# Own-chunk values of an attention layer computed transposed, with the head mask summed by ScalarE and VectorE

## The chip, the cores and the metric

The kernel runs on one core of a Trainium2 chip. The metric is the device time of one launch in microseconds (us), lower is better.

## The reference

Four layers follow one another. The first two are a scan layer with a gate and eight small experts, the third is a linear attention over 16 heads, the fourth is a gated cell that carries a state through 16 batches of 512 tokens of 128 features. Only the attention's sum over earlier tokens is touched:

```python
scores = jnp.einsum('bthd,bshd->bhts', Q, K) * S ** (-0.5)
Wmat = scores * jnp.transpose(decay, (0, 3, 1, 2)) * jnp.transpose(lam_ts, (0, 2, 1, 3))
Y = jnp.einsum('bhts,bshd->bthd', Wmat, V).reshape(Bb, Tt, H * HD)
o = Y @ Wout.T + x
```

H is 16 heads, a head's value has 8 features (HD), lam_ts depends on the level of the pair (t, s) in a binary tree. The part in which t and s lie in the same chunk of 32 tokens is what is changed here.

## The kernel before

A batch is four tiles of 128 tokens. The kernel is written engine by engine, with every wait spelled out as a semaphore. Each engine runs `stages(i, j)`, in which the attention and cell of batch i are interleaved with the scan and expert layers of batch j = i + 1: once for batch 0, 14 times in a hardware loop, then `last()` for batch 15. The order in each engine's queue is the order written in its `stages`; it is in this order that a waiting instruction holds up all that stands behind it.

**The attention of one batch.** Pairs across chunks go through node matrices: `levels` (L733 and L737 on TensorE, PE) makes products that VectorE (DVE) weights (`level_products`, L1732) and sums (`level_total`, L1739). Pairs in the same chunk: `pair_scores` (L702) gives scores, `pair_weights` (L1718) multiplies them in place into `pair`, 128 partitions of (chunk, s) by 16 heads x 32 tokens for each tile. Then for each tile n
- `chunk_values` (L748): four matmuls, four heads each, with `pair` as the stationary operand and `vbd` moved, a copy of the values in which each chunk has its own columns (filled by four ScalarE copies of 32 partitions, L1149). The result holds (head, token) on partitions, and of its columns only those of the partition's own head are wanted;
- `own_heads` (L1750): DVE multiplies the 512 columns by a head mask into `ym`;
- `chunk_sums` (L756): four matmuls with a matrix of ones sum the four heads away, so that tokens stand on partitions;
- `tile_sum` (L1761): DVE adds the level sums, into `yt`.

`turn_out` (L765) transposes `yt`, ScalarE (ACT) copies it (L1203), `project_out` (L771) multiplies with Wout, and `attention_out` (L1766) adds the skip path. `norm2` (L1467 with skip as output) normalises the batch before; GpSimd (POOL) then runs `finish` and `residual(i)`, and `sum0` (L1573) waits for the latter.

**The steps around it.** PE runs `levels(i, 3)`, which waits for `level_products(i, 2)`, and directly behind it `out0(j)` (L559 to L563). `sum0` and `norm1` on DVE follow, then `turn_x1` (L574) on PE, the gates of the cell (L784 to L793), the copy x1Th on ACT (L1095, waits for the third gate), `low_part` (L1587) on DVE, `values` (L582 to L590) on PE, the cell, the next `norm0` and its two short ACT steps (L1014), the gates `gates1` up to `g_ready`, `running_sums` (L634 and L637), `token_sums` (L1677), and so on to `delta` on DVE (L1531), for which `scan_b` (L501 with MBCl) waits. `heads` (L626 to L628) are 48 matmuls per batch in split fp32 (high and low part as fp32r), each with an ACT copy (L1115). `deltas` (L493) is one plain fp32 matmul per batch; the trace counts every plain fp32 matmul as two instructions.

**Start and end.** `node_vectors` builds small coefficient columns on DVE at the end of `first()`; POOL's `split_weights` (L2026, L2028) makes the high and low parts of five weight blocks before the loop. At the end POOL and DVE add the last outputs (L2064, L1799) and SyncE (SP) stores them; the two halves of batch 15 wait for `last_out` (L1906) behind `last_norm` (L1896).

```python
for g in range(4):
    at = 512 * n + 128 * g
    mm = pe.matmul(tile(P1[3], g), pair[:, at:at + 128], vbd[:, at:at + 128], start=True, stop=True)
```

Of the kernel before, what the change touches and what calls it, by code (L numbers as in the profile page):

```python
# [29 lines left out]
NODES = 32  # L30
EPS = 1e-5
# [33 lines left out]
def build(nc, x, weights, consts, out):  # L65
# [9 lines left out]
    with ExitStack() as ctx:  # L75
# [50 lines left out]
        Mdelta = sb("Mdelta", 128)  # L126
# [69 lines left out]
        with nc.sbuf_tensor("cellh", [128, T], fp32r) as cellh, nc.sbuf_tensor("celll", [128, T], fp32r) as celll:  # L196
# [9 lines left out]
        vbd = sb("vbd", TILES * 512)  # L206
# [6 lines left out]
        ym = sb("ym", 2 * 512)  # L213
        dts = pair[:, 0:12 * 64]
        lvs = sb("lvs", 128)
        cgt = lvs[:, 0:64]
# [23 lines left out]
        P1 = [psum(f"p1_{n}") for n in range(5)]  # L240
# [13 lines left out]
            s_ps lam_ps dlam_ready w_ready vbd_zero vbd_ready y1_ps ym_ready y2_ps lev_ps lev_ready levsum_ready  # L254
# [31 lines left out]
        def _(sp):  # L286
# [49 lines left out]
            def last():  # L336
# [16 lines left out]
                for b in (0, 1, 2, 3, 4, 7, 8, 9, 10, 5, 6, 11, 12):  # L353
                    if b in END_POOL:
                        sp.wait_ge(R["end_pool_add"], END_POOL.index(b) + 1)
                    else:
                        sp.wait_ge(R["end_add"], END_DVE.index(b) + 1)
                    store(b, whole, end_hx[b])
                for half in range(2):
                    sp.wait_ge(R["end_add"], len(END_DVE) + 1 + half)  # L360
                    store(B - 1, slice(2 * half, 2 * half + 2), end_hx[B - 1])
                    sp.wait_ge(R["end_pool_add"], END_POOL.index(13 + half) + 1)
                    store(13 + half, whole, end_hx[13 + half])
# [5 lines left out]
        def _(pe):  # L369
# [122 lines left out]
            def deltas(j):  # L492
                pe.matmul(P0[0][:, :], Mdelta[:, :], xnT[:, :], start=True, stop=True).then_inc(R["delta_ps"], 1)  # L493
# [17 lines left out]
            def scan_x(j):  # L511
                if later(j):
                    pe.wait_ge(R["wsplit_steps"], 10)
# [20 lines left out]
            def gate_u(j, q):  # L534
# [7 lines left out]
                else:  # L542
                    pe.wait_ge(R["hsplit_ready"], 2 * j)
# [33 lines left out]
            def values_in_parts(j):  # L577

                pe.wait_ge(R["x1P_ready"], j + 1)
                for n, free in enumerate(("dlam_ready", "ym_ready", "yt_ready", "x1Th_ready")):  # L580
                    pe.wait_ge(R[free], j + 1 if n == 3 else 4 * j)
                    pe.matmul(P1[(2 + n) % 5][:, 336:VDW], tile(x1P, n), w("Wvdw", 336, VDW), start=True, stop=True)  # L582
                pe.wait_ge(R["wsplit_steps"], 10)
# [9 lines left out]
            def values(j):  # L593
# [5 lines left out]
                for n, free in enumerate(("dlam_ready", "ym_ready", "yt_ready", "x1Th_ready")):  # L599
# [30 lines left out]
            def running_sums(i):  # L630
# [3 lines left out]
                pe.matmul(P1[2][:, 0:64], upto[:, :], g, start=True, stop=False)  # L634
                pe.wait_ge(R["gsum_steps"], 2 * i + 2)
# [104 lines left out]
            def chunk_values(i, n):  # L740
                if n > 0:
                    pe.wait_ge(R["ym_ready"], 4 * i + n)
# [3 lines left out]
                for g in range(4):  # L746
                    at = 512 * n + 128 * g
                    mm = pe.matmul(tile(P1[3], g), pair[:, at:at + 128], vbd[:, at:at + 128], start=True, stop=True)  # L748
                mm.then_inc(R["y1_ps"], 1)

            def chunk_sums(i, n):
                if n > 0:
                    pe.wait_ge(R["yt_ready"], 4 * i + n)
                pe.wait_ge(R["ym_ready"], 4 * i + n + 1)
                for c in range(4):
                    mm = pe.matmul(P1[4][32 * c:32 * c + 32, 0:128], k("sum_heads"),  # L756
                                   view(tile(ym, n % 2, 512), "p (g c v) -> p g c v", g=4, c=4)[:, :, c, :],
                                   start=True, stop=True)
                mm.then_inc(R["y2_ps"], 1)
# [28 lines left out]
            def recur_cell(i, n):  # L788

                pe.wait_ge(R["csplit_ready"], 2 * i + 2)  # L790
# [5 lines left out]
            def stages(i, j):  # L796
# [41 lines left out]
                if i is not None:  # L838
                    chunk_sums(i, 0)
# [8 lines left out]
                if i is not None:  # L848
                    chunk_sums(i, 1)
# [5 lines left out]
                if i is not None:  # L855
                    chunk_sums(i, 2)
                if i is not None:
# [3 lines left out]
                if i is not None:  # L861
                    chunk_values(i, 3)
                    if j is not None:
# [1341 lines left out]
```

## Time and profile before

| | |
|---|---|
| median of 3 runs | 1022.07 us (1021.91 to 1022.53) |
| profiled execution, own time | 1022.31 us |
| its span, first to last instruction | 1020.5 us |
| PE busy | 969.2 us (95%) |
| DVE busy | 858.9 us (84%) |
| ACT busy | 704.3 us (69%) |
| POOL busy | 254.9 us (25%) |
| granted TensorE clock, mean | 0.990 |

Busy time counts overlapping matmuls once. Some 1.8 us of the profiled execution lie outside the span.

### The profile page before, as it was taken

How to read it: one execution, taken by the hardware profiler on the slowest of the kernel's cores; microseconds unless marked ns; L12 is line 12 of the kernel's file. 1: busy time of each engine (PE TensorE's matmuls, PEld its weight loads, DVE VectorE, ACT ScalarE, POOL GpSimd, SP SyncE). 2: the span in 40 equal slices, each digit the busy share in tenths (PEclk: the TensorE clock that was granted, in tenths of full speed). 3: DMA queues.
4: the chain of work that ended last, by engine and by line, in shares of the span. 5: the costliest groups of instructions: out<-in, count | busy, mean ns of one | idle time of the engine just before them, and what ended most of it. 6: DMA issues, size and time to landing. Idle time of an engine off the chain costs nothing. (4 is left out here: it accounts for less than half of the span.)

```text
span 1020.5 us, 20931 instructions
## 1 busy us (share of the span) xinstructions
PE 969.2 (95%) x6894; PEld 708.1 (69%) x6894; DVE 858.9 (84%) x2156; ACT 704.3 (69%) x1528; POOL 254.9 (25%) x319
## 2 busy tenths in 40 slices
PE   6879999999999999999999999999999999999995
PEld 3656767767676777768677676766767677776763
DVE  6888797988979798897979979798897979889777
ACT  4575784939579494866939577593957849396684
POOL 0042021220222122021312212132122212202367
PEclk9989999999999999999999999999999999999997
DMA  4000000000000000000000000000000000000526
GB/s 159 18 4 1 22 2 23 8 21 10 0 31 0 21 10 10 21 0 31 0 21 10 0 31 0 31 0 21 10 0 31 0 21 10 10 21 0 196 77 202
DMA packets 31909, 27.62 MB, mean 27 GB/s; under 512 B 1553, under 2 KB 25745, under 8 KB 31761
## 3 DMA queue, kind: packets, MB, share of 16 engines
q1 hardware_dynamic: 31888, 27.37, 8.3%
q8 instruction: 11, 0.18, 0.1%
q14 instruction: 10, 0.07, 0.0%
HBM read 15.57 MB, written 11.80 MB: 27 GB/s over the span
## 5 line engine op out<-in xcount | busy, mean ns | idle before, releaser
L1115 ACT ACTIVATE gx<-p 128x512 f32<-128x512 f32 x256 | 146.5, 597 | 2.1 <-PE p L628 0.5
L626 PE MATMUL p<-x1Th,Gl 128*128 128x512 f32 x256 | 107.7, 421 | 0.0
L628 PE MATMUL p<-x1Th,Gh 128*128 128x512 f32 x256 | 101.4, 396 | 0.0
L627 PE MATMUL p<-x1Tl,Gh 128*128 128x512 f32 x256 | 100.6, 393 | 0.0
L1979 POOL TENSOR_TENSOR vp<-vdw,e 128x256 f32<-128x256 f32 (+3 forms) x80 | 55.1, 724 | 162.3 <-DVE ms L1663 162.3
L1063 ACT ACTIVATE gelu<-p,bias_u 128x512 f32<-128x512 f32 x32 | 22.0, 688 | 105.3 <-PE p L550 105.3
L748 PEld LDWEIGHTS p<-vbd,pair 128*128 128x128 f32 x512 | 62.0, 191 | 40.4 <-issue 26.8
L748 PE MATMUL p<-vbd,pair 128*128 128x128 f32 x512 | 73.3, 286 | 0.0
L2040 POOL TENSOR_TENSOR skip<-skip,W 128x512 f32<-128x512 f32 x15 | 19.2, 1279 | 215.4 <-DVE skip L1467 215.4
L688 PEld LDWEIGHTS p<-rs,GT 128*128 128x128 f32 x512 | 60.7, 191 | 16.8 <-ACT ms L1198 14.6
L1069 ACT ACTIVATE sm<-mv 128x4 f32<-128x4 f32 x31 | 6.3, 204 | 91.4 <-DVE mv L1462 91.0
L702 PE MATMUL p<-gx,x1T 128*32 128x512 f32 x512 | 67.8, 602 | 0.2 <-DVE pair L1718 0.2
L1991 POOL TENSOR_TENSOR xnTl<-xnT 128x1 fp32r<-128x1 f32 x15 | 2.9, 194 | 248.6 <-DVE pair L1618 248.6
L688 PE MATMUL p<-rs,GT 128*128 128x120 f32 x512 | 63.8, 278 | 0.2 <-ACT ms L1198 0.2
L1704 DVE TENSOR_TENSOR pair<-pair,p 128x512 f32<-128x512 f32 x64 | 42.5, 684 | 24.9 <-PE p L719 24.9
L628 PEld LDWEIGHTS p<-x1Th,Gh 128*128 128x128 f32 x256 | 48.3, 189 | 11.0
L1198 ACT ACTIVATE ms<-p 128x120 f32<-128x120 f32 x256 | 46.9, 287 | 11.3 <-PE p L688 8.8
L626 PEld LDWEIGHTS p<-x1Th,Gl 128*128 128x128 f32 x256 | 48.7, 190 | 8.3 <-ACT gx L1115 0.7
L627 PEld LDWEIGHTS p<-x1Tl,Gh 128*128 128x128 f32 x256 | 48.7, 190 | 7.6
L1750 DVE TENSOR_TENSOR ym<-p,K 128x512 f32<-128x512 f32 x64 | 43.7, 683 | 2.7 <-PE p L748 2.7
L737 PE MATMUL p<-ms,x1T 128*128 128x128 f32 x256 | 45.5, 300 | 0.0
L1739 DVE TENSOR_REDUCE lvs<-lv 128x128 f32<-128x256 f32 (+1 forms) x64 | 43.2, 675 | 2.2
(340 smaller groups left out, 2855.6 us busy)
## 6 DMA issues: line engine op xcount, KB each, us to landing
xin<-in_x SPq DMA_DIRECT2D x16, 256.0 KB, 2.8
hx_scratch<-vdw SPq DMA_DIRECT2D x15, 256.0 KB, 2.6
res_scratch<-normed SPq DMA_DIRECT2D x14, 256.0 KB, 2.0
gx<-in_weights SPq DMA_DIRECT2D x1, 1216.0 KB, 9.4
vp<-hx_scratch SPq DMA_DIRECT2D x4, 256.0 KB, 3.8
GT<-res_scratch SPq DMA_DIRECT2D x4, 256.0 KB, 3.4
out<-vp SPq DMA_DIRECT2D x4, 256.0 KB, 3.5
W<-in_weights SPq DMA_DIRECT2D x1, 746.0 KB, 10.5
```

What stands on the lines that cost most here:

```text
L626: pe.matmul(head_bank(h)[:, :], tile(Gl, h), x1Th[:, :], start=True, stop=False)
L627: pe.matmul(head_bank(h)[:, :], tile(Gh, h), x1Tl[:, :], start=False, stop=False)
L628: pe.matmul(head_bank(h)[:, :], tile(Gh, h), x1Th[:, :], start=False, stop=True).then_inc(R["gx_ps"], 1)
L688: mm = pe.matmul(bank[:, 120 * a:120 * a + 120], tile(GT, h), view(rs[:, 0:1920], "p (n c) -> p n c", c=128)[:, :, HD * h:HD * h + HD], st ...
L702: mm = pe.matmul(P1[1][32 * c:32 * c + 32, :], x1T[:, 128 * n + 32 * c:128 * n + 32 * c + 32], view(gx[:, :], "p (h t) -> p h t", h=H)[:, ...
L737: mm = pe.matmul(bank[:, 128 * (a + 1):128 * (a + 2)], tile(x1T, n), node(m), start=True, stop=True)
L748: mm = pe.matmul(tile(P1[3], g), pair[:, at:at + 128], vbd[:, at:at + 128], start=True, stop=True)
L1115: act.activation(tile(gx, h, T), head_bank(h)[:, :], ACT.Copy).then_inc(R["gx_copied"], 1)
L1198: cp = act.activation(dst[:, at], src[:, at], ACT.Copy)
L1739: dve.tensor_reduce(lvs[:, :], view(lv[:, 0:128 * count], "p (l v) -> p v l", l=count), AX.X, ALU.add)\
L1750: dve.tensor_tensor(view(tile(ym, n % 2, 512), "p (m a e) -> p m a e", m=16, a=4), view(P1[3][:, :], "p (m a e) -> p m a e", m=16, a=4), s ...
L1979: last = pool.tensor_tensor(view(vp[:, at:at + 128 * count], "p (s h e) -> p s h e", s=count, e=HD), spread(v.unsqueeze(1), [128, count, H ...
```

## The change

The own-chunk product is taken with the operands exchanged. The values are now the stationary operand (64 partitions of two chunks by 32 columns, four heads of 8), `pair` moves with the weights of four heads (128 columns), and 16 matmuls per tile write features on partitions and tokens on columns, in the two banks `y1`. Each partition needs one of four column blocks, the one of its own head: ACT takes the first with a mask as its scale (`first_part`), DVE adds the three others (`other_parts`). The result `yc` is already transposed, so the level sums go alone through `turn_out`, and DVE adds `yc` after it (`turned_out`) in place of the ACT copy. `vbd` is filled by two ACT copies of 128 partitions. With it: `deltas` becomes three fp32r matmuls with a broadcast column, the running sums are cut in two around a head, `left_ends` goes ahead of `deltas`, `turn_out` ahead of the gates, `norm2` ahead of the third tile; part of `node_vectors` and the POOL splits move into stage 0; the end of the kernel keeps its last tiles in PSUM and stores in another order.

```diff
+PARTS = 4
+PASSES = 4 // PARTS
...
+        y1 = ctx.enter_context(nc.psum_tensor("p1_34", [128, 1024], fp32))
+        P1 += [y1[:, 0:512], y1[:, 512:1024]]
+        def quadrant_part(a):
+            return view(y1[:, :], "p (h x) -> p h x", h=2)[:, :, 64 * a:64 * a + 64]
+        def by_token(ap):
+            return view(ap, "p (h x) -> p h x", h=2)
...
             def deltas(j):
+                column = lambda t: spread(t[:, 0:1], [128, 128])
...
+                pe.wait_ge(R["wsplit_steps"], 6)
+                pe.wait_ge(R["xsplit_ready"], 2 * j)
+                pe.matmul(P0[0][:, :], column(Mdl), xnTh[:, :], start=True, stop=False)
+                pe.matmul(P0[0][:, :], column(Mdh), xnTl[:, :], start=False, stop=False)
+                pe.matmul(P0[0][:, :], column(Mdh), xnTh[:, :], start=False, stop=True).then_inc(R["delta_ps"], 1)
...
             def chunk_values(i, n):
                 if n > 0:
-                    pe.wait_ge(R["ym_ready"], 4 * i + n)
+                    pe.wait_ge(R["yc_ready"], 4 * i + n)
...
-                for g in range(4):
-                    at = 512 * n + 128 * g
-                    mm = pe.matmul(tile(P1[3], g), pair[:, at:at + 128], vbd[:, at:at + 128], start=True, stop=True)
+                width = CHUNK * PARTS
+                for c in range(2):
+                    for b in range(PASSES):
+                        for half in range(2):
+                            rows = slice(64 * half, 64 * half + 64)
+                            for g in range(4):
+                                at, of = 32 * (((4 * n + g) * 2 + c) * PASSES + b), 512 * n + 128 * g + width * b
+                                to = view(P1[3 + half][32 * g:32 * g + 32, 0:2 * width], "p (a c t) -> p a c t", a=PARTS, c=2)
+                                mm = pe.matmul(to[:, :, c], vbd[rows, at:at + 32],
+                                               view(pair[rows, of:of + width], "p (a t) -> p a t", a=PARTS),
+                                               start=(b == 0), stop=(b == PASSES - 1))
...
-            def chunk_sums(i, n):
...
                     heads(i, 7, 8)
+                    carried_sums(i)
                 if j is not None:
                     logits(j)
+                if i is not None:
+                    left_ends(i)
+                if j is not None:
                     deltas(j)
                 if i is not None:
-                    left_ends(i)
                     heads(i, 8, 12)
...
                     chunk_values(i, 3)
+                    turn_out(i)
...
-                    chunk_sums(i, 3)
...
-                    turn_out(i)
...
+            def first_part(i, n):
+                act.wait_ge(R["y1_ps"], 4 * i + n + 1)
+                act.activation(by_token(yu[:, :]), quadrant_part(0), ACT.Copy, scale=head_part[:, 0:1]).then_inc(R["yu_ready"], 1)
...
-            def own_heads(i, n):
...
-            def tile_sum(i, n):
...
+            def other_parts(i, n):
+                dve.wait_ge(R["yu_ready"], 4 * i + n + 1)
+                for a in range(1, PARTS):
+                    if a > 1:
+                        dve.wait_ge(R["yc_steps"], (PARTS - 2) * (4 * i + n) + a - 1)
+                    last = dve.scalar_tensor_tensor(by_token(tile(yc, n)), quadrant_part(a), head_part[:, a:a + 1],
+                                                    by_token(yu[:, :] if a == 1 else tile(yc, n)), ALU.mult, ALU.add)
+                    last.then_inc(R["yc_ready" if a == PARTS - 1 else "yc_steps"], 1)
+
+            def turned_out(i):
+                dve.wait_ge(R["ytT_ps"], i + 1)
+                dve.wait_ge(R["yc_ready"], 4 * i + 4)
+                dve.tensor_tensor(ytT[:, :], P1[1][:, :], yc[:, :], ALU.add).then_inc(R["ytT_ready"], 1)
...
-                    own_heads(i, 0)
                     pair_weights(i, 1)
+                    other_parts(i, 0)
                     level_sum(i, 0)
-                    tile_sum(i, 0)
                 if j is not None:
                     gate0(j, 0)
...
                     gate0(j, 1)
                 if i is not None:
-                    own_heads(i, 2)
-                    level_sum(i, 2)
                     if later(i):
                         norm2(i - 1)
+                    other_parts(i, 2)
+                    level_sum(i, 2)
                     pair_weights(i, 3)
-                    tile_sum(i, 2)
                     level_sum(i, 3)
...
+            last_ob = P1[3]
...
+            def split_scan_weights():
+
+                pool.wait_ge(R["z1_ps"], 1)
+                pool.wait_ge(R["xh_ready"], 2)
+                split_weights(((Mdh, Mdl, Mdelta[:, :]), (Winh, Winl, w("Win")), (MBCh, MBCl, MBC[:, :])), 0)
+
+            def split_other_weights():
+
+                pool.wait_ge(R["u1_ps"], 1)
```

The lines left out: `node_vectors` now runs ahead of `gates_low_part` in `first()`; its second half, `node_coefficients`, with five short instructions more for the new masks, runs in stage 0 ahead of `fold_own`. ACT's `stages` calls `first_part(i, n)` ahead of the gate's tanh, between tanh and gelu, between the two gelus, and behind them. In `last()` ACT copies the first head ahead of `rstd2` and runs `lam_logs` behind the fourth, the last output tile of batch 15 is built in the bank `P1[3]` (in L1879, L1896, L1906), and SP stores batches 13 and 14 ahead of the two halves of batch 15.

## Rows read from the trace of the kernel before

**Rows 1.** The page, busy time by engine.
```profile
PE 969.2 (95%) x6894; PEld 708.1 (69%) x6894; DVE 858.9 (84%) x2156; ACT 704.3 (69%) x1528; POOL 254.9 (25%) x319
```

**Rows 2.** Groups of PE: count | busy us, mean ns | idle before, releaser.
```profile
L748 PE MATMUL p<-vbd,pair 128*128 128x128 f32 x512 | 73.3, 286 | 0.0
...
L719 PE MATMUL p<-nodesT,K 32*32 32x512 f32 x512 | 34.8, 599 | 0.4 <-DVE pair L1704 0.4
...
L756 PE MATMUL p<-ym,K 128*32 128x128 f32 x512 | 27.3, 284 | 6.1 <-DVE ym L1750 6.1
```

**Rows 3.** Groups of DVE.
```profile
L1750 DVE TENSOR_TENSOR ym<-p,K 128x512 f32<-128x512 f32 x64 | 43.7, 683 | 2.7 <-PE p L748 2.7
...
L1761 DVE TENSOR_TENSOR rs<-lvs,p 128x128 f32<-128x128 f32 x64 | 18.3, 286 | 12.6 <-PE p L756 9.4
```

**Rows 4.** Timeline of DVE in one period: start us, us, what [idle before].
```profile
503.37 0.69 DVE L1704 TENSOR_TENSOR pair<-pair,p 128x512 f32<-128x512 f32 x1 [0.92 <-PE p L719]
...
507.07 1.28 DVE L1704 TENSOR_TENSOR pair<-pair,p 128x512 f32<-128x512 f32 x2 [0.35 <-PE p L719]
...
521.84 0.61 DVE L1732 TENSOR_TENSOR lv<-p,alpha 128x256 f32<-128x256 f32 x2
...
523.00 1.11 DVE L1467 TENSOR_SCALAR skip<-skip,mv,sm 128x128 f32<-128x128 f32 x4
...
528.43 0.69 DVE L1573 TENSOR_TENSOR x<-p,xin 128x512 f32<-128x512 f32 x1 [1.82 <-POOL res L1965]
...
535.66 0.69 DVE L1587 TENSOR_TENSOR x1Tl<-x1T,x1Th 128x512 fp32r<-128x512 f32 x1 [1.90 <-ACT x1Th L1095]
...
553.82 0.68 DVE L1531 SCALAR_TENSOR_TENSOR decay<-p,sp 128x512 f32<-128x512 f32 x1
```

**Rows 5.** Timeline of PE in the same period.
```profile
522.70 0.44 PE L733 MATMUL p<-ms,x1T 128*64 128x128 f32 x4
...
523.85 0.39 PE L559 MATMUL p<-W,y 128*128 128x128 f32 x2
...
527.75 0.22 PE L563 MATMUL p<-b_b,oh_b 128*128 128x128 bf16 x1
...
532.38 0.63 PE L574 MATMUL p<-K,xn 128*128 128x128 f32 x4 [0.68 <-DVE xn L1467]
...
545.88 0.42 PE L637 MATMUL p<-pair,ones 128*128 128x48 f32 x2 [0.41 <-DVE pair L1624]
...
547.37 1.13 PE L493 MATMUL p<-xnT,Mdelta 128*128 128x512 f32 x2
...
554.97 0.39 PE L501 MATMUL p<-xnTh,MBCl 128*128 128x512 f32 x1
...
555.66 0.39 PE L501 MATMUL p<-xnTh,MBCl 128*128 128x512 f32 x1
```

**Rows 6.** Timeline of ACT in the same period.
```profile
535.03 0.60 ACT L1095 ACTIVATE x1Th<-p 128x512 fp32r<-128x512 f32 x1 [0.48 <-PE p L793]
...
540.56 0.21 ACT L1014 ACTIVATE sm<-sm 128x4 f32<-128x4 f32 x1 [0.43 <-DVE sm L1482]
```

**Rows 7.** Timelines at the start: DVE twice, then PE.
```profile
49.42 1.27 DVE L1413 SCALAR_TENSOR_TENSOR K<-K 128x128 f32<-128x128 f32 x1
...
53.59 3.04 DVE L1467 TENSOR_SCALAR xn<-xin,mv,sm 128x128 f32<-128x128 f32 x4
...
56.78 1.08 PE L467 MATMUL p<-K,xn 128*128 128x128 f32 x4 [5.50 <-DVE xn L1467]
```

**Rows 8.** Timelines at the end: DVE twice, then POOL, then SP's queue.
```profile
1012.62 2.16 DVE L1896 SCALAR_TENSOR_TENSOR skip<-skip,mv,W 128x128 f32<-128x128 f32 x2
...
1015.40 0.61 DVE L1896 SCALAR_TENSOR_TENSOR skip<-skip,mv,W 128x128 f32<-128x128 f32 x2
...
1013.11 1.26 POOL L2064 TENSOR_TENSOR W<-W,normed 128x512 f32<-128x512 f32 x1
...
1017.16 0.49 SPq L333 DMA_DIRECT2D out<-W  x1
```

More of the change, by code:

```diff
@@ L358, in last @@
                     store(b, whole, end_hx[b])
+                for b in (13, 14):
+                    sp.wait_ge(R["end_pool_add"], END_POOL.index(b) + 1)
+                    store(b, whole, end_hx[b])
                 for half in range(2):
@@ L1219, in end_tanh @@
                 act.activation(END_BANKS[turn][:, :] if b in END_DVE else end_hx[b], end_hx[b], ACT.Tanh).then_inc(R["end_tanh"], 1)
-            def last_copy(half, bank):
-                act.wait_ge(R["ytT_ps"], B + half)
-                act.activation(ytT[:, 256 * half:256 * half + 256], bank[:, 0:256], ACT.Copy).then_inc(R["ytT_ready"], 1)
             def last_rstd(half):
@@ L1280, in stages @@
                 gelus()
+                if i is not None:
+                    first_part(i, 0)
                 if j is not None:
@@ L1405, in node_vectors, with node_coefficients @@
                 step(last)
+            def node_coefficients():
+                step(dve.tensor_tensor(chunk_part[:, :], k("own_chunk", 0, 2), k("own_chunk", 2, 4), ALU.add))
+                for a in range(PARTS):
+                    step(dve.tensor_reduce(head_part[:, a:a + 1], view(k("diag"), "p (b x) -> p b x", b=PASSES)[:, :, 8 * a:8 * a + 8],
+                                           AX.XY, ALU.add))
                 step(dve.memset(ones_to[:, 0:1], 1.0))
@@ L1445, in first @@
                 later_weights()
+                node_vectors()
                 gates_low_part()
@@ L1737, in level_total @@
                 dve.wait_ge(R["lev_ready"], 4 * i + n + 1)
+                if n == 0 and later(i):
+                    dve.wait_ge(R["ytT_ps"], i)
                 count = sum(r[2] for r in level_runs(n))
-                dve.tensor_reduce(lvs[:, :], view(lv[:, 0:128 * count], "p (l v) -> p v l", l=count), AX.X, ALU.add)\
-                    .then_inc(R["levsum_ready"], 1)
+                dve.tensor_reduce(tile(yt, n), view(lv[:, 0:128 * count], "p (l v) -> p v l", l=count), AX.X, ALU.add)\
+                    .then_inc(R["yt_ready"], 1)
             def level_sum(i, n):
@@ L1818, in stages @@
                     lam_sum(i)
+                    if not later(i):
+                        node_coefficients()
                     fold_own(i)
@@ L1848, in stages @@
                 if i is not None:
-                    own_heads(i, 1)
                     pair_weights(i, 2)
+                    other_parts(i, 1)
                     level_sum(i, 1)
-                    tile_sum(i, 1)
                 if j is not None:
@@ L1866, in stages @@
                 if i is not None:
-                    own_heads(i, 3)
-                    tile_sum(i, 3)
+                    other_parts(i, 3)
+                    turned_out(i)
                 if j is not None:
@@ L1872, in stages, with last_turned @@
                     recurrence(i)
+            last_ob = P1[3]
+            def last_turned(half, bank):
+                cols = slice(256 * half, 256 * half + 256)
+                dve.wait_ge(R["ytT_ps"], B + half)
+                dve.wait_ge(R["yc_ready"], 4 * (B - 1) + 2 * half + 2)
+                dve.tensor_tensor(ytT[:, cols], bank[:, 0:256], yc[:, cols], ALU.add).then_inc(R["ytT_ready"], 1)
             def last_attention_out(half):
@@ L1884, in last_stats @@
                 for n in (2 * half, 2 * half + 1):
-                    last = dve.bn_stats(st2[:, 6 * n:6 * n + 6], tile(ob, n))
+                    last = dve.bn_stats(st2[:, 6 * n:6 * n + 6], tile(last_ob, n))
                 last.then_inc(R["st2_ready"], 1)
@@ L2083, in stages @@
             def stages(i, j):
+                if not later(i):
+                    split_scan_weights()
                 split_inputs(j)
@@ L2086, in stages @@
                 split_rows(i, j)
+                if not later(i):
+                    split_other_weights()
                 split_cell(i, 2 * i + 2)
```

145 lines of the change are left out of this document (66 added, 79 removed).

## The prediction

> **What bounds the kernel now.** I read the busy times first: PE has 95% and DVE 84% of the span [rows 1], so PE looks like the bound. The groups of PE by line then show what the change can take from it, and their idle column that PE waits for DVE there, 6.1 us in all before L756 [rows 2]. Last the timelines of the three engines over one period, to see which wait ends last. The reader is to see two stretches. From 507.07 DVE works without a gap until level_total of tile 3 [rows 4], and PE runs just behind it: `out0` starts at 523.85 [rows 5]. From `out0` to the copy x1Th the batch is one chain through PE, DVE and ACT, with idle time on each (1.82, 0.68, 1.90 us [rows 4, 5]). So both engines are at their limit in the first stretch, and in the second latency counts, not load. A faster PE gets only as far as DVE's queue lets it.
>
> **PE, removed and added.** One tile's `chunk_values` takes 73.3 / 64 = 1.15 us and its `chunk_sums` 27.3 / 64 = 0.43 [rows 2], together 6.3 us per batch. The new product issues 32 instructions per tile (16 fp32 matmuls of two) on eight places of the array, two row halves by four column groups. The nearest row for eight places is L719: 16 instructions of 512 columns take 34.8 / 32 = 1.09 us, so eight run at once. For 128 columns the nearest is L756: eight instructions on four places, two rounds, in 0.43. Four rounds of eight then cost about twice that less one start, 0.65 us; if only four ran at once, eight rounds, 1.4 us; a quarter of L719's time scaled, 0.5, is the lower end. I take 0.65, as L719 has both row and column places. By TensorE: Matmul & The Clock Gate, The mechanism, of the Trainium skill, weights load beside running matmuls only where the row groups differ, which would put the four column groups of one half in a row and the price at the upper end. L756 lies all in one row group and still takes 0.43 for eight, so I leave the price.
>
> `deltas` is 1.13 us busy now [rows 5]. Three fp32r matmuls start 0.23 apart (the six from 554.97 to 555.66 and on: 0.69 for three [rows 5]), about 0.8 with the start: 0.2 less. PE thus loses some 3.9 us of work per batch, 60 us over the kernel. What follows says how much of it arrives.
>
> **ACT.** The four masked first parts cost about 0.3 us each and lie in its waits for the gate; `own_values` falls from four instructions to two and the copy of `ytT` goes. Nothing here is on the path; if it were, the two would nearly cancel. Cost taken as nothing, cover: ACT waits behind norm statistics and gelu, 69% busy [rows 1].
>
> **DVE, where the sum is made.** `own_heads` is 0.683 us long [rows 3], but independent instructions of 512 columns follow one another every 0.60 (two in 1.28 [rows 4]). `tile_sum` is 0.286 [rows 3] and with the gap before it adds 0.38. In their place stand three dependent instructions of 128 columns with a pointer scalar. The nearest is L1896, two in 0.61 [rows 8]: 0.35 long, 0.26 apart when independent. Dependent, each of the first two costs 0.35 + 0.04, the last 0.26: 1.04 per tile. Bounds: 0.28 each without the pointer's share gives 0.85; 0.45 each, should two banks in one operand cost more, gives 1.3. Up to `level_products` of tile 2, DVE now does 3 x 1.04 instead of 3 x 0.60 + 2 x 0.38, +0.56, and the moved `norm2`, 1.02 of its 1.11 [rows 4], stands ahead of it: +1.6. In the old order it ends at 521.84 + 0.61 = 522.45 [rows 4] and PE takes `levels(3)` at 522.70 [rows 5]; in the new one both are at 524.1. PE, some 3 us early, waits, and `out0` stands behind that wait. **`out0` is 1.4 us late.**
>
> **What the rest of the period gives back.** Each as a shift against the old timeline:
> - `sum0`: `out0` ended at 527.75 + 0.22 = 527.97, `sum0` began at 528.43 behind POOL's `res` [rows 4, 5]. POOL is started by `norm2`, now earlier, so 0.4 is given back: +1.0. The same for `turn_x1` (532.38 [rows 5]). `chunk_values(3)` and `turn_out` fit ahead of it: 0.65 + 0.43 instead of 1.1, with 0.68 idle.
> - The third gate follows without the 0.36 of `chunk_sums(3)`: +0.64 for x1Th (535.03 [rows 6]) and `low_part` (535.66 [rows 4]). The moved `turn_out` would take 0.43 more off `values`, but its fourth block waits for x1Th: heads enter at about +0.3.
> - The cell and `norm0` follow on DVE; ACT's next gated step, idle 0.43 before it at 540.56 [rows 6], comes at +0.57, and so does `g_ready`.
> - PE no longer idles 0.41 before L637 [rows 5], since a head stands between, but the head (0.7) delays the sums by 0.3: `token_sums` at +0.87. PE itself is level with the old timeline here, with the 0.2 of `deltas`.
> - `delta` on DVE ends at 553.82 + 0.68 = 554.50 [rows 4], at +0.87 is 555.37. `scan_b` was at 554.97 [rows 5]. PE waits: **+0.45**. DVE's own 0.87 vanishes in its 0.92 idle at 503.37 [rows 4], PE's 0.45 does not.
>
> So a period is 0.45 us longer, and 14 of them and the last half one make +6.6 us.
>
> **Start.** PE waits 5.50 us for xn of batch 1 at 56.78 [rows 7], behind `node_vectors` (its last piece at 49.42) and four normalising instructions that take 3.04 instead of 1.11 while POOL splits weights [rows 4, 7]. Both leave that place. But `node_coefficients`, some 4.1 us with its five new instructions, comes back ahead of `fold_own` in stage 0, where DVE has under 1 us idle, and POOL's split now stands beside the gates, where it can hold DVE as it did before. Gain 2.0 us, between 0 and 4. By the GPSIMD Engine Reference of the Trainium skill POOL contends with Vector instructions that have two SBUF inputs; the gates have such ones, so by the rule the stall moves rather than ends, and 2 rather than 4 is right.
>
> **End.** The last store is issued at 1017.16 [rows 8], behind the halves of batch 15, though POOL is done at 1013.11 + 1.26 = 1014.37. It now goes ahead. On DVE the three-part sums add 0.3 in all plus two sums of 0.33, while `last_norm` reads PSUM: 0.61 instead of 2.16 [rows 8]; DVE also had waits at the start of its last tiles. It ends about 1.6 us earlier, and the last store moves by 2.4 us (1.2 if the 2.16 stays).
>
> **Sum.** Against the profiled execution, 1022.31 us: + 6.6 - 2.0 - 2.4 = 1024.5; the median is 0.24 lower, so 1024.3 us.
>
> **Rivals.**
> - *The three-part sum is cheap (faster).* With 0.85 per tile the shift of `out0` is 0.8, the pause at `scan_b` goes, and a period is about 0.15 shorter: 14.5 x -0.15 = -2.2, with start and end -6.6: about 1015.5. For it: dependent short steps elsewhere on DVE cost little more than their length. Against: the pointer's 0.07 shows in L1896. It decides at 0.90 per tile, where a period is unchanged; start and end alone then give 1017.9. Chance 0.33, with all cases below 1020.
> - *The DVE chain costs more (clearly slower).* 1.3 per tile: + 0.8 on `out0` and as much per period, about 1033. Chance 0.1.
> - *Four places at once, not eight.* 1.4 us per tile: hidden in tiles 0 to 2 by PE's new slack, but `chunk_values(3)` stands between `out0` and `turn_x1`, and passes the 0.68 idle by 0.4: +6, about 1030. Chance 0.05.
> - *PE's saving arrives* because DVE has a gap I don't see: a third of 60 us, about 1005. Chance 0.03. DVE's unbroken stretch speaks against it.
> - *Nothing much*: loop +2 to +6 cancelled by start and end, 1020 to 1024. Chance 0.22.
>
> **Numbers.** 0.2% is 2 us, about what a measurement of this kernel can tell. Slower by more, with my forecast, 0.44; within, 0.22; faster, 0.34. Eight in ten: from 1013 to 1031, which takes in the cheap sum and leaves out the 1.3 and the full saving.
>
> **What would show it.** In the changed profile PE should idle before `levels` of tile 3, about 3 us per batch, with DVE's `level_products` as the releaser, and a little before `scan_b`, released by `delta`. Its busy share falls to about 88%. The 32 instructions of a tile should span 0.65 us plus tails, the three DVE instructions 1.04. `sum0` should wait for PE instead of POOL, the first xn on PE should come 4 to 5 us earlier, and the last store should be of batch 15. The prediction is wrong at its root if PE doesn't wait at `levels(3)`, and in its size if the three-part sum isn't 1.04.

## The result, and the profile after

The changed kernel takes 1053.51 us, the median of four runs (1052.30 to 1055.19), against 1022.28 us for the kernel before in the same rounds (1021.91 to 1022.53): a ratio of 1.0304, 95% interval 1.0288 to 1.0321. It is 3% slower. The forecast was 1024.3 us with a range up to 1031.0, so the true time lies far outside. One of the four runs of e1 below (1031.58 us) and one of the kernel before beside it (1070.28 us) were slow ones, at a granted clock of 0.85: the medians count them, the ratios don't.

The page of the changed kernel gives busy times, and below them the clock that TensorE was granted, slice by slice.

```profile
span 1051.7 us, 23196 instructions
PE 951.7 (90%) x7933; PEld 692.3 (66%) x7933; DVE 877.1 (83%) x2242; ACT 698.8 (66%) x1543; POOL 254.0 (24%) x321
...
PEclk9989999999999998999999999998999999899997
```

The summary by core (us from first to last instruction, mean granted clock):

```profile
core 0: 1051.7 us, clock 0.957
```

PE's share fell from 95% to 90% [rows 1], yet its busy time fell only 17.5 us, not the 60 us that the prediction takes out. The mean clock is the first thing to see: 0.957, where the kernel before had 0.990. The page's digits nearly hide it, since a short fall is averaged over a slice of 26 us.

The groups of PE and DVE (count | busy us, mean ns | idle before):

```profile
L782 PE MATMUL p<-pair,vbd 64*32 64x128 f32 x2048 | 43.7, 279 | 0.4
L760 PE MATMUL p<-ms,x1T 128*64 128x128 f32 x256 | 30.4, 317 | 47.0 <-DVE lv L1771 47.0
L524 PE MATMUL p<-xnTh,MBCl 128*128 128x512 f32 x60 | 25.3, 422 | 0.4 <-DVE decay L1568 0.4
...
L1792 DVE SCALAR_TENSOR_TENSOR yc<-p,head_part,yc 128x128 f32<-128x128 f32 x128 | 44.9, 350 | 4.5
```

`chunk_values` costs 43.7 / 64 = 0.68 us a tile instead of 1.15 [rows 2], and `chunk_sums` is gone. In their place stands the wait of `levels` (L760): 47.0 us for DVE's level values, 3.15 us in each of 14 batches, as forecast, and 1.64 and 1.21 in the first and the last.

The same moments as in [rows 4, 5], one batch of the changed kernel: DVE (L1741 is the reference, at 507.07 before), then PE.

```profile
521.56 1.28 DVE L1741 TENSOR_TENSOR pair<-pair,p 128x512 f32<-128x512 f32 x2 [0.35 <-PE p L746]
...
535.81 1.11 DVE L1504 TENSOR_SCALAR skip<-skip,mv,sm 128x128 f32<-128x128 f32 x4
536.84 0.34 DVE L1792 SCALAR_TENSOR_TENSOR yc<-p,head_part,yu 128x128 f32<-128x128 f32 x1
537.22 0.74 DVE L1792 SCALAR_TENSOR_TENSOR yc<-p,head_part,yc 128x128 f32<-128x128 f32 x2
537.87 0.61 DVE L1771 TENSOR_TENSOR lv<-p,alpha 128x256 f32<-128x256 f32 x2
...
545.35 0.69 DVE L1610 TENSOR_TENSOR x<-p,xin 128x512 f32<-128x512 f32 x1 [2.62 <-PE p L587]
```

```profile
538.62 0.69 PE L760 MATMUL p<-ms,x1T 128*64 128x128 f32 x4 [3.15 <-DVE lv L1771]
539.25 1.65 PE L764 MATMUL p<-ms,x1T 128*128 128x128 f32 x6
540.69 0.63 PE L583 MATMUL p<-W,y 128*128 128x128 f32 x2
...
543.14 0.44 PE L583 MATMUL p<-W,y 128*128 128x128 f32 x2
```

PE waits 3.15 us, and then the same instructions are longer: L760 takes 0.69 us where it took 0.44 [rows 5], and L583 takes 0.63 in its first pair and 0.44 two rounds later. Stretches of the same batch (us | busy PE, PEld, DVE, ACT, POOL | PEclk) say why:

```profile
534.00:538.30 4.30, 1.47 (x11) 0.98 (x11) 4.12 (x12) 1.97 (x2) 1.26 (x1) 1.00 0.00 0
538.30:541.70 3.40, 3.08 (x15) 2.78 (x16) 2.10 (x5) 0.00 (x0) 3.09 (x3) 0.50 0.20 77
541.70:545.30 3.60, 3.60 (x41) 3.41 (x44) 1.03 (x1) 0.00 (x0) 0.00 (x0) 1.00 0.00 0
```

Behind the wait the granted clock is 0.50, that is 1.2 GHz, from 538.3 to 541.7, and 1.00 (2.4 GHz) again afterwards. Each of the 14 waits of 3.15 us has such a fall of the clock, for 3.4 us in nine batches and 6.8 us in five. The five long ones begin 0.5 to 1.1 us before the wait ends, the nine short ones from 0.4 us before its end to 1.0 us behind it. Two more falls of 3.4 us have other places: one at 91.2, behind a wait of 2.31 us of L729 in the first batch, one at 1036.7, behind the 1.21 us of the last. So the loop is longer than anything in the forecast's sum. The group of the transposes that begin each batch's node matrices gives the mean period:

```profile
L1708 DVE STREAM_TRANSPOSE nodesT<-ms x16: 2302/2311/2312, 72.7 to 1015.3; 128x2048 f32<-128x2048 f32 x16
```

(1015.3 - 72.7) / 15 = 62.84 us. The kernel before has (982.4 - 73.1) / 15 = 60.62:

```profile
L1671 DVE STREAM_TRANSPOSE nodesT<-ms x16: 2302/2312/2314, 73.1 to 982.4; 128x2048 f32<-128x2048 f32 x16
```

Leaving out the first and the last, single periods are 60.44 to 60.49 us before; after they are 62.2 to 62.4 with a short fall of the clock and 63.4 to 63.7 with a long one.

### The profile page after: what moved, and what is told of

Its sections match the earlier page's. It is cut to its first block and busy times, and to the rows that moved or that the text cites. A ratio compares the mean times of both kernels' runs of the same rounds, so it can differ in the third digit from the quotient of the medians.

```text
span 1051.7 us, 23196 instructions
## 1 busy us (share of the span) xinstructions
PE 951.7 (90%) x7933; PEld 692.3 (66%) x7933; DVE 877.1 (83%) x2242; ACT 698.8 (66%) x1543; POOL 254.0 (24%) x321
## 5 line engine op out<-in xcount | busy, mean ns | idle before, releaser
L1180 ACT ACTIVATE yu<-p,head_part 128x128 f32<-128x128 f32 x64 | 23.5, 368 | 189.0 <-PE p L782 188.9
L729 PE MATMUL p<-gx,x1T 128*32 128x512 f32 x512 | 68.8, 610 | 15.6 <-DVE pair L1755 15.3
L760 PE MATMUL p<-ms,x1T 128*64 128x128 f32 x256 | 30.4, 317 | 47.0 <-DVE lv L1771 47.0
L715 PEld LDWEIGHTS p<-rs,GT 128*128 128x128 f32 x512 | 60.7, 191 | 15.6 <-ACT ms L1226 13.4
L1741 DVE TENSOR_TENSOR pair<-pair,p 128x512 f32<-128x512 f32 x64 | 42.4, 684 | 23.6 <-PE p L746 23.6
L782 PEld LDWEIGHTS p<-pair,vbd 64*32 64x32 f32 x2048 | 27.1, 107 | 45.0 <-issue 45.0
L764 PE MATMUL p<-ms,x1T 128*128 128x128 f32 x256 | 55.5, 352 | 0.0
L760 PEld LDWEIGHTS p<-ms,x1T 128*64 128x64 f32 x256 | 14.0, 144 | 59.0 <-issue 59.0
L1610 DVE TENSOR_TENSOR x<-p,xin 128x512 f32<-128x512 f32 x16 | 11.1, 691 | 49.7 <-PE p L587 49.7
```

The lines of the kernel that those rows point to most:

```text
L715: mm = pe.matmul(bank[:, 120 * a:120 * a + 120], tile(GT, h), view(rs[:, 0:1920], "p (n c) -> p n c", c=128)[:, :, HD * h:HD * h + HD], st ...
L729: mm = pe.matmul(P1[1][32 * c:32 * c + 32, :], x1T[:, 128 * n + 32 * c:128 * n + 32 * c + 32], view(gx[:, :], "p (h t) -> p h t", h=H)[:, ...
L760: pe.matmul(bank[64 * c:64 * c + 64, 0:128], x1T[:, 128 * n + 64 * c:128 * n + 64 * c + 64], node((2 * n, 8 + n)[c]), start=True, stop=True)
L764: mm = pe.matmul(bank[:, 128 * (a + 1):128 * (a + 2)], tile(x1T, n), node(m), start=True, stop=True)
L782: mm = pe.matmul(to[:, :, c], vbd[rows, at:at + 32], view(pair[rows, of:of + width], "p (a t) -> p a t", a=PARTS), start=(b == 0), stop=(b ...
L1741: dve.tensor_tensor(tile(pair, n, 512), tile(pair, n, 512), P1[(2, 0)[n % 2]][:, :], ALU.mult)\
```

## The experiments

Theory T: PE's wait of 3 us ahead of `levels(3)`, made by the order of DVE's queue, makes the clock fall, and that is most of the loss. R1: the clock falls for another reason and DVE's longer queue is the loss. R2: the new form of matmul (64 x 32 places) lowers the clock. The ratio is to the kernel before in the same rounds. In the table "period" is that of steady batches without a fall / with a 3.4 us one, "falls" counts them in the loop's last 14 periods, and the wait is PE's longest that recurs in them. e7 leaves out a part of the sum, so its output is another one; all the others compute the same.

| kernel | median us | ratio to before, 95% | PE's wait | falls | period |
|---|---|---|---|---|---|
| before | 1022.28 | 1 | 0.7 | 0 | 60.46 |
| changed | 1053.51 | 1.0304 (1.0288 to 1.0321) | 3.15 | 14 | none / 62.38 |
| e1, reordered | 994.75 | 0.9731 (0.9711 to 0.9750) | 1.10 | 0 | 58.69 |
| e2, wait filled | 1025.75 | 1.0037 (1.0024 to 1.0050) | 0.77 | 0 | 60.74 |
| e3, norm2 back | 1033.09 | 1.0094 (1.0065 to 1.0122) | 2.13 | 13 | 60.27 / 61.37 |
| e4, old kernel delayed | 1080.80 | 1.0577 (1.0559 to 1.0595) | 2.6 | 11 | 63.40 / 64.50 |
| e5, old kernel reordered | 1056.14 | 1.0323 (1.0305 to 1.0340) | 2.0 | 6 | 62.11 / 63.73 |
| e6, e1 with products first | 1006.09 | 0.9833 (0.9817 to 0.9850) | 0.9 | 0 | 59.43 |
| e7, e1 with one part less | 983.75 | 0.9622 (0.9606 to 0.9638) | 0.8 | 0 | 57.95 |
| e8, wait half filled | 1033.94 | 1.0111 (1.0094 to 1.0128) | 1.72 | 5 | 60.76 / 62.41 |
| e9, e1 with old deltas | 997.12 | 0.9746 (0.9729 to 0.9763) | 1.1 | 0 | 58.81 |
| e10, e1 with norm2 late | 1033.50 | 1.0113 (1.0097 to 1.0128) | 2.19 | 5 | 60.87 / 62.43 |
| e11, e1 again | 995.25 | 0.9739 (0.9726 to 0.9752) | 1.1 | 0 | 58.70 |

### e2: the wait filled with work

```diff
                 if i is not None:
+                    for _ in range(12):
+                        pe.matmul(P1[2][:, :], tile(Gh, 0), x1Th[:, :], start=True, stop=True)
                     levels(i, 3)
```

> Edit: the changed kernel, with 12 fp32r matmuls of 128 columns (tile 0 of Gh by x1Th, into the third bank of P1, which the next batch's values overwrite; the output is unchanged) ahead of levels(3) of each batch, some 2.8 us of work in a wait of 3.15 us. Theory T: PE has more to do and ends its wait at the same moment, but the clock stays at 1.0: a period loses the 1.4 to 2.9 us that the stretches at 0.5 cost, and the kernel takes 1022 to 1030 us. Rival R1 (DVE's longer queue alone costs the time): work laid into a wait changes nothing, 1053 us, or some us more. Rival R2 (the form of the new matmuls lowers the clock): the stretches at 0.5 stay, 1053 us.

The matmuls stream 512 columns each, not 128 as that text calls them. 1025.75 us: adding 3 us of work to the busiest engine in 15 of the 16 batches saves 28 us. The wait and what follows (timeline of PE), then the stretches around it:

```profile
523.16 3.01 PE L884 MATMUL p<-x1Th,Gh 128*128 128x512 f32 x12
526.51 0.44 PE L760 MATMUL p<-ms,x1T 128*64 128x128 f32 x4 [0.34 <-DVE lv L1773]
526.88 0.94 PE L764 MATMUL p<-ms,x1T 128*128 128x128 f32 x6
527.65 0.39 PE L583 MATMUL p<-W,y 128*128 128x128 f32 x2
```

```profile
526.00:529.50 3.50, 3.16 (x28) 2.83 (x28) 3.17 (x6) 0.00 (x0) 3.18 (x4) 1.00 0.19 75
529.50:533.00 3.50, 3.50 (x58) 3.11 (x58) 1.33 (x5) 0.37 (x1) 0.10 (x1) 1.00 0.00 0
```

`levels(3)` is released by the same DVE instruction as in the changed kernel and at the same point of DVE's queue, but now runs at full clock. R1 and R2 both wanted 1053. This run also prices the change without the clock: the period is 60.74 us, 0.28 more than before.

### e4: the wait put into the old kernel

```diff
                 if i is not None:
+                    for n in range(5):
+                        dve.tensor_reduce(pad[:, n:n + 1], spread(w("lng").unsqueeze(1), [128, 4, 128]), AX.XY, ALU.add)
                     own_heads(i, 2)
```

> Edit: the kernel before, with five reductions of 512 columns on DVE (their results go nowhere) ahead of own_heads(2), some 2.8 us. It has none of the 64x32 matmuls. PE then waits some 3 us before levels(3), as in the changed kernel. Theory T: the granted clock falls to 0.5 behind this wait, in the old kernel too, and a period costs 1.4 to 2.9 us more than the delay itself; with 1 to 2.5 us of delay arriving at the end of the period, that gives 60.5 + 2.4 to 5.4 per period, 1058 to 1100 us. R1 (the queue alone): at most the 2.8 us of added work per period, 1022 + 42 = 1064, with the clock at 1.0 in the loop. R2 (the new form of matmul lowers the clock): the clock stays at 1.0 here.

The stretches of one batch of e4, around a wait of 2.62 us ahead of L757 (`chunk_sums`, where the delay of `own_heads` meets PE first; the expectation had placed it at `levels(3)`):

```profile
487.74 0.43 PE L757 MATMUL p<-ym,K 128*32 128x128 f32 x8 [2.62 <-DVE ym L1751]
```

```profile
486.00:489.50 3.50, 1.66 (x19) 1.28 (x20) 3.46 (x10) 1.15 (x1) 0.00 (x0) 1.00 0.00 0
489.50:492.90 3.40, 3.40 (x18) 3.30 (x17) 2.74 (x6) 0.00 (x0) 2.72 (x3) 0.50 0.00 0
```

The old kernel, which has none of the new matmuls, loses the clock in the same way, in 11 of 14 periods. R2 falls here too. Periods without a fall are 2.94 us longer than before (the added work; 1 to 2.5 us of it were expected to arrive), those with one 1.1 us more. R1 had a ceiling of 1064 us; 1080.8 is above it, but most of that is the added work, 15 x 2.94 = 44 of the 58.5 us, and the falls of the clock are 11 x 1.1 = 12. What rules R1 out is the clock at 0.50, not the time alone.

### e1: the order of DVE's queue, and its repeat e11

```diff
                 if i is not None:
+                    level_products(i, 2)
                     if later(i):
                         norm2(i - 1)
+                    level_total(i, 2)
                     other_parts(i, 2)
-                    level_sum(i, 2)
                     pair_weights(i, 3)
```

> Edit: the changed kernel with DVE's queue reordered behind gate0 of the second half: level_products(2) first, then norm2 and level_total(2), then other_parts(2). That brings the level values of tile 2, on which PE waits before levels(3), forward by norm2 and other_parts, 1.02 + 1.03 = 2.05 us. Theory T (PE's wait of 3.15 us there makes the granted clock fall to 0.5 behind it): the wait shrinks to some 1.1 us, TensorE's clock stays at 1.0 in every batch, a period falls from 62.2 to 63.7 us to between 60.0 and 60.7, and the kernel takes 1013 to 1023 us. Rival R1 (the clock falls for another reason, only the longer queue of DVE is undone): the stretches at 0.5 stay, a period gets at most the 2 us of the shorter wait, and the kernel stays above 1030 us. Rival R2 (the 64x32 matmuls themselves lower the clock): as R1, the granted clock stays at about 0.957 on average.

994.75 us, and 995.25 in the repeat, is faster than either theory said. It is 2.7% faster than the kernel before and 5.6% faster than the changed one (994.75 / 1053.51 = 0.944), with the same computation. The summary, the group, and DVE's timeline of one batch:

```profile
core 0: 992.5 us, clock 0.990
```

```profile
L1708 DVE STREAM_TRANSPOSE nodesT<-ms x16: 2300/2311/2314, 71.7 to 956.1; 128x2048 f32<-128x2048 f32 x16
```

```profile
509.16 0.61 DVE L1771 TENSOR_TENSOR lv<-p,alpha 128x256 f32<-128x256 f32 x2
509.69 1.10 DVE L1504 TENSOR_SCALAR skip<-skip,mv,sm 128x128 f32<-128x128 f32 x4
510.71 0.59 DVE L1780 TENSOR_REDUCE rs<-lv 128x128 f32<-128x384 f32 x1
511.21 0.34 DVE L1792 SCALAR_TENSOR_TENSOR yc<-p,head_part,yu 128x128 f32<-128x128 f32 x1
...
515.22 0.69 DVE L1610 TENSOR_TENSOR x<-p,xin 128x512 f32<-128x512 f32 x1 [0.58 <-PE p L587]
```

The level products of tile 2 stand first, 1.02 + 1.03 us earlier. The gain of 31 us over e2 is nearly all this: the period went from 60.74 to 58.69, 2.05 us, what the products moved by, and 15 periods of that are 30.8 us. The expected 60.0 to 60.7 was too high: `sum0` is released by PE 0.58 us after DVE is free, and POOL's `res`, which `norm2` starts early, doesn't hold it.

> The first experiment's kernel once more, unchanged, beside these two in the same rounds: 993 to 997 us, 2.5 to 2.9% under the kernel before.

As expected: 995.25 us.

### e3 and e8: how long a wait the clock bears

```diff
 # e3
-                    if later(i):
-                        norm2(i - 1)
                     other_parts(i, 2)
                     level_sum(i, 2)
+                    if later(i):
+                        norm2(i - 1)
                     pair_weights(i, 3)
 # e8, the diff of e2 with
+                    for _ in range(6):
```

> Edit: the changed kernel with norm2 back in its old place, behind level_sum(2). The level values of tile 2 come 1.02 us earlier, so PE waits some 2.1 us ahead of levels(3), between the 0.25 of the kernel before and the 3.15 of the changed one. Theory T has no row for a wait of this length: either the clock falls as often as now and the kernel gains 0 to 15 us (1038 to 1053), or it falls in fewer batches or none, 1018 to 1030. Rival R1: about 1 us per period less, 1038, with the clock as it is. R2: the same as R1. The run says which waits the clock bears, and tells R1 apart only together with the first and the fourth.

> Edit: as the second experiment, but with 6 dummy matmuls ahead of levels(3) instead of 12 (the changed kernel otherwise), some 1.4 us of work, so PE idles 1.7 us there. The runs so far bear 1.1 us (the clock stays at 1.0) and not 2.1 (the clock falls in nearly every batch, for 3.4 us). Theory T in the form that the idle stretch decides: at 1.7 us either no stretch at 0.5 in the loop, a period of 60.74 us and 1026 us, or one in most batches, about 61.9 us and 1040. Rival (the half clock is cured by the number of matmuls, not by the idle time, in proportion): the stretches at 0.5 last half as long on average, 1040 us. The median alone does not tell these apart; the list of stretches does.

e3, with 2.13 us, falls in 13 of 14 periods; the one without takes 60.27 us, those with 61.37 (leaving out the last, which is some 2 us longer in every kernel). Its 1033.09 us meets neither branch of its expectation: the clock falls about as often as in the changed kernel, yet the gain is 20.4 us and not 0 to 15, since all these falls are short and cost 1.1 us each. e8, with 1.72 us, falls in 5 of 14: those periods have about 62.4 us, again without the last, and the nine others about 60.8. Neither line of the last expectation is met, for the clock falls neither in most batches nor in none. All its falls in the loop last 3.4 us, so the fillers cure some batches wholly and others not at all.

```profile
528.34 0.44 PE L760 MATMUL p<-ms,x1T 128*64 128x128 f32 x4 [1.72 <-DVE lv L1773]
```

```profile
529.10:532.50 3.40, 3.40 (x18) 3.34 (x18) 2.08 (x3) 0.00 (x0) 2.14 (x3) 0.51 0.20 77
```

The length of the one wait isn't the whole rule: e4 with 2.6 us falls less often than e3 with 2.1. Even one program differs from execution to execution: in the first batch of e1 and of its repeat e11 PE waits 2.3 us ahead of L729, and the clock falls behind it at 91.2 in e11 and not at all in e1. What else decides was not separated. That wait and the stretch behind it, e1 first, then e11:

```profile
89.89 1.06 PE L729 MATMUL p<-gx,x1T 128*32 128x512 f32 x8 [2.32 <-DVE pair L1755]
90.50:94.50 4.00, 3.21 (x59) 1.93 (x55) 3.84 (x8) 1.05 (x2) 0.00 (x0) 1.00 0.00 0
```

```profile
90.35 1.13 PE L729 MATMUL p<-gx,x1T 128*32 128x512 f32 x8 [2.30 <-DVE pair L1755]
91.20:94.60 3.40, 3.40 (x46) 2.38 (x43) 3.26 (x7) 0.37 (x1) 0.00 (x0) 0.50 0.00 0
```

### e5: the good order in the old kernel

```diff
-                    own_heads(i, 2)
-                    level_sum(i, 2)
+                    level_products(i, 2)
                     if later(i):
                         norm2(i - 1)
+                    level_total(i, 2)
+                    own_heads(i, 2)
```

> Edit: the kernel before with the queue order of the first experiment: behind gate0 of the second half level_products(2), norm2, level_total(2), then own_heads(2). The question is whether the gain of that order belongs to the change or was to be had without it. Theory D (in the kernel before PE is the bound, waiting only 0.25 us before levels(3); the order pays only where PE has slack): a period falls by 0 to 0.25 us from 60.46, or grows by some tenths as PE's chunk_sums(2) now waits for own_heads(2); 1018 to 1030 us. Rival O (the order alone brought it, and the old kernel would gain as much): a period of 58.7 us, some 995 us.

1056.14 us, worse than both expectations. In the old kernel PE's `chunk_sums(2)` needs `own_heads(2)`, and moved behind, it holds PE where the changed kernel has nothing to wait for:

```profile
L756 PE MATMUL p<-ym,K 128*32 128x128 f32 x512 | 27.3, 283 | 35.1 <-DVE ym L1750 35.1
```

That was 6.1 [rows 2]. So rival O is out: this order gains only together with the change. Another order of the old kernel, say `level_products(2)` first and `own_heads(2)` ahead of `norm2`, was not run, so how much of the 2.7% needs the change isn't settled. In the old kernel this order costs 1.65 us per period without a fall, and the clock falls in 6 of 14 besides.

### e6, e7, e9, e10: what bounds the reordered kernel

e6 puts `level_products(i, 2)` ahead of `gate0(j, 1)` also; e7 loops `for a in (1, 3)` in `other_parts` (its wait between them counts one step per tile instead of two); e9 takes the old body of `deltas`; e10 moves `norm2(i - 1)` behind `pair_weights(i, 3)`.

```diff
 # e6
                 if i is not None:
                     level_products(i, 2)
+                if j is not None:
+                    gate0(j, 1)
 # e7
-                for a in range(1, PARTS):
+                for a in (1, 3):
 # e10
-                    if later(i):
-                        norm2(i - 1)
                     level_total(i, 2)
                     other_parts(i, 2)
                     pair_weights(i, 3)
+                    if later(i):
+                        norm2(i - 1)
```

> Edit: the first experiment's kernel with other_parts summing two of its three masked parts (the one of column group 2 is left out, so the output lacks that part); one DVE instruction of 128 columns less per tile, four per batch. It measures what the three dependent sums are worth where they stand on the path. By the step of the prediction (0.35 + 0.04 us each, two ahead of level_products(2), PE behind it): 0.8 us per period, 57.9 us, 983 us in all. Rival (DVE has slack once the clock holds, PE is the bound again): under 0.2 us per period, 992 to 995 us.

983.75 us and a period of 57.95: 0.74 less for the two instructions ahead of `level_products(2)`, 0.37 each. The prediction's price was 0.39, and nearly all of it is on the path. DVE's queue up to that point bounds the reordered kernel.

> Edit: the first experiment's kernel, with level_products(2) also ahead of gate0 of the second half. In that run PE finishes levels(2) at 507.9 where DVE would ask for it at 507.1, and it waits 1.10 us ahead of levels(3). Expected: that wait of PE goes, DVE gets a new one of about 0.5 us, out0 now waits for gate0 instead and starts 0.1 to 0.7 us earlier; a period of 58.0 to 58.6 us against 58.69, 985 to 993 us, the clock at 1.0. If DVE's queue in front of sum0 is the true bound, the new wait of DVE costs its 0.5 us and the kernel comes out at 1000 us.

1006.09 us, a period of 59.43. PE's wait at `levels(3)` went, but DVE now waits 0.7 us for PE's levels (10.9 us in all), and PE waits elsewhere:

```profile
PE p L598 <- DVE xn L1504: 13.0, 15, 0.9
PE p L583 <- issue: 11.3, 15, 0.8
```

The second branch of the expectation has the right sign and is too small: 1000 us were said, a wait of 0.5 and not 0.7 us. The period grew by 0.74 us, the wait's length: what DVE waits ahead of `sum0` is worth more than what PE waits at `levels(3)`.

> Edit: the first experiment's kernel with norm2 three calls later, behind level_total(2), other_parts(2) and pair_weights(3). The prediction had POOL's res (started by norm2) as the end of the wait before sum0 in the kernel before, 5.4 us from norm2 to sum0. Theory: norm2 comes some 2.1 us later, so sum0 waits for POOL again, at 5.4 us behind norm2, 2 us later than now: a period of 60.7 us and 1022 to 1027 us, the clock at 1.0 unless PE's wait before turn_x1 lengthens to 2 us. Rival (POOL has slack in the new order): DVE's queue up to level_products(3) is the same length, so nothing changes, 995 us.

1033.50 us; the period without a fall is 60.87, against 60.7 expected. POOL's `res` ends the wait before `sum0` again, and PE's wait before `turn_x1` (L598) grows to 2.19 us; the clock falls behind that wait in 5 of 14 periods. So a second place, with another releaser, shows the same fall. The waits (engine, what <- whom: us in all, times, longest):

```profile
DVE x L1610 <- POOL res L2013: 36.9, 14, 2.6
```

```profile
475.96 1.04 PE L598 MATMUL p<-K,xn 128*128 128x128 f32 x4 [2.19 <-DVE xn L1504]
```

> Edit: the first experiment's kernel with deltas in its old form, one fp32 matmul of 512 columns instead of three fp32r ones. By the prediction's term (1.13 us instead of 0.8): 0.35 us more on PE's queue ahead of scan_x and scan_b. If the chain there goes through PE, the whole of it arrives, 15 x 0.35 = +5 us, 1000 us; if it goes through DVE's delta and decay, nothing, 995 us.

997.12 us against e11's 995.25, with runs from 993.39 to 997.91, so the times hardly tell the two apart. The traces do: the period is 0.12 us longer, so a third of the 0.35 arrives, and `deltas` is mostly beside the path.

## Why the prediction was wrong

**The step that failed** is "PE, some 3 us early, waits, and `out0` stands behind that wait. `out0` is 1.4 us late." The wait is there, 3.15 us, with the releaser named. It was priced as a wait alone. Behind it TensorE runs at 1.2 GHz for 3.4 or 6.8 us, and since it has no slack there, the lost time reaches the end of the period. By e2 this costs 62.84 - 60.99 = 1.85 us in the mean period, (1053.51 - 1025.75) = 27.8 us in all; the miss was 29.2. No rival had it either: every one moved waits about and left each matmul as long as in the rows of before. The rows to ask for were there. In the kernel before no recurring wait of PE is longer than 0.7 us (0.68 in [rows 5]), so its durations hold for a PE that hardly pauses; the one long wait behind its first microseconds, 5.50 us up to 56.78 [rows 7], ends in a stretch at 0.50 (the row below, from the windows of the kernel before), and the L467 behind it takes 1.08 us where L574, of the same form, takes 0.63 [rows 5].

```profile
54.10:60.90 6.80, 4.12 (x14) 3.56 (x15) 6.02 (x20) 4.44 (x11) 2.93 (x5) 0.50 0.00 1
```

By the Trainium skill (TensorE: Matmul & The Clock Gate, HAM oscillation — how this bites in real kernels) a wait (there for a transfer) that recurs in every tile of a matmul kernel throws the clock back in every tile. The trace agrees in kind, with a fall at each of 14 waits of 3.15 us, here for DVE.

Step by step, with e2 as the changed kernel at full clock (reference L1741, there L1743, at 509.44):

- `chunk_values` 0.65 us a tile: 0.68. Eight places run at once; the rival of four places is out, and so is the upper price by the rule on weight loads that the prediction names. (L756's stationary operand has all 128 rows; its places differ by column only.)
- The three-part sum 1.04 us: 536.84 to 537.87 in the changed kernel, 1.03. Both rivals on its price are out (1.3 us a tile would have been 14.5 x 0.8 = 11.6 above 1024.3, some 1036, and not the 1033 that the prediction gives), and e7 shows its weight.
- `deltas` 0.8 us: right in size (L514 to the next in 0.78), nearly weightless by e9.
- `out0` +1.4: in e2 at 527.65, 18.21 behind the reference against 16.78 [rows 4, 5], +1.43.
- `sum0` +1.0: in e2 at 531.81, 22.37 against 21.36 [rows 4], +1.01, released by PE and not POOL, as forecast.
- `low_part` +0.64: 538.44, 29.00 against 28.59, +0.41. The turn of the sums fitted in better.
- The period +0.45: +0.28 in steady batches; the "little wait before `scan_b`" isn't there: L524 waits 0.4 us in all. In its stead PE waits 0.45 us for ACT's copy of a head (the row below, from e2), on an engine whose cost the prediction took as nothing. Behind `deltas` PE is 0.45 us ahead of the old timeline, and 0.19 behind it at the next L524; that ACT's queue sets this was not tested. In the mean over all 15 periods the growth is 60.99 - 60.62 = +0.37, so the loop takes 5.5 us where the prediction has 6.6, for 14.5 periods.
- Start -2.0: too much. The first L1708 comes at 72.7 (72.3 in e2), against 73.1 before. Over all profiles it is 71.5 to 72.9 in ten with the new start and 71.8 to 73.5 in three with the old, so the gain is hardly clear of the spread. The xn of batch 1 starts at 49.77 instead of 53.59 [rows 7], and PE takes it at 51.14 instead of 56.78, but POOL's split now stands beside DVE's small instructions of 64 columns, two of which take 1.3 us instead of 0.22, and PE waits 2.42 us behind the second. "The stall moves rather than ends" was right, and the gain of 2.0 still too hopeful. Their rows are below, from DVE's timeline, and under them what POOL did meanwhile: they lie beside its two subtractions. Of the small instructions beside its casts L1653 grew too, to 0.52 us, the others keep their 0.22.
- End -2.4: from the last L1708, 36.4 us instead of 38.1, -1.7 (-1.6 in e2). The term for `last_norm` was right: with its operand in PSUM its two instructions take 0.59 us beside POOL instead of 2.16 [rows 8].

```profile
553.95 0.50 PE L650 MATMUL p<-x1Th,Gl 128*128 128x512 f32 x1 [0.45 <-ACT gx L1140]
```

```profile
53.64 1.29 DVE L1651 TENSOR_TENSOR pair<-pair 128x64 f32<-128x64 f32 x1
54.97 0.52 DVE L1653 SCALAR_TENSOR_TENSOR pair<-pair 128x64 f32<-128x64 f32 x1
55.52 1.31 DVE L1655 TENSOR_TENSOR pair<-pair,neg_a 128x64 f32<-128x64 f32 x1
```

```profile
53.56 1.29 POOL L2071 TENSOR_TENSOR Winl<-W,Winh 128x512 fp32r<-128x512 f32 x1
54.80 0.61 POOL L2069 CAST MBCh<-MBC 128x512 fp32r<-128x512 f32 x1
55.48 1.27 POOL L2071 TENSOR_TENSOR MBCl<-MBC,MBCh 128x512 fp32r<-128x512 f32 x1
```

By the GPSIMD Engine Reference of the Trainium skill (Key points) POOL contends with Vector instructions in a 2-port perf mode or with two SBUF inputs. The two of 1.3 us have such inputs and agree, and so does `last_norm`, which had two and now has one. In the kernel before the four xn, with one tensor as input each, took 3.04 us beside the split [rows 7]; whether they ran in such a mode no run here shows.

At full clock the sum is 5.5 - 0.8 - 1.6 = +3.1 us against the profile, and e2's median is 1025.75 us where 1024.3 was said. So the forecast was right to 1.5 us for a clock that holds, and in part by luck: the loop was put 1.1 us too high, the start and the end 1.2 and 0.8 us too low. The other 27.8 us of the miss are the clock.

## What to carry to other kernels

When a change takes work from the engine that was always busy, and the next engine's queue now makes it wait, price two things: the wait, and what the wait does to the engine's clock. Then look at the order of the other engine's queue before judging the change, since here two lines moved in DVE's order turned 3% slower into 2.7% faster (e1); put first what the waiting engine needs, and leave early what a third engine needs (`norm2`, e10). If the wait can't be removed, dummy matmuls in it pay for themselves (e2), though here they only bring the kernel back to the time before (1.0037).

## What was unexpected of the hardware

- The clock fell to 0.50 at recurring waits of PE as short as 1.72 us (e8, 5 of 14 periods), and not at those of 1.10 us (e1, e9, e11). Length alone doesn't decide how often: 1.99 us fell in 6 of 14 (e5), 2.13 in 13 (e3), 2.19 in 5 (e10), 2.6 in 11 (e4), and one wait of 1.21 us, in the last batch of the changed kernel, had a fall too.
- One fall of 3.4 us costs 1.1 us (e3, e4) to 1.65 us (e8; 1.64 in the changed kernel, 62.38 against e2's 60.74).
- Work that computes nothing, on the engine with the highest load, made the kernel 2.6% faster (e2 against the changed kernel, 1025.75 / 1053.51).
